# Two attention layers and the stage between them put into one block, with loads, weights and first steps moved inside the stage ahead

## The reference

```
x = x + L0_xattn(layernorm(x), ctx)   # attention, 16 heads of 16; every weight W becomes W + 2 * A @ B
x = x + sqrt(real^2 + imag^2)         # real = layernorm(x) @ cos(theta + theta_noise)
                                      # imag = layernorm(x) @ sin(phi + phi_noise)
x = x + L1_xattn(layernorm(x), ctx)   # attention, 16 heads of 16, queries and keys rotated by position
x = x + L1_ffn(layernorm(x))          # 256 -> 1024 -> 256, gelu, weights rounded to 8 bits, activations to 16
```

## Time and profile before

| what | us |
|---|---|
| median of 3 runs | 1995.51 (1990.53 to 1996.17) |
| the profiled execution | 1991.47 |
| its span, from the first instruction to the last | 1989.7 |
| busy: PE, DVE, ACT, POOL | 1665.4, 1316.0, 1219.0, 831.3 |
| granted TensorE clock, mean share of full speed | 0.91 |
| end of the chain of waits by engine: DMA, DVE, PE, ACT | 4%, 2%, 2%, 1% |

### The profile page before, as it was taken

One profiled execution on the slowest core, in us unless ns is written; L12 is line 12 of the kernel. 1 busy time (PEld: TensorE's weight loads), 2 busy tenths in 40 slices (PEclk: granted clock), 3 DMA queues, 4 the chain that ended last, 5 costly groups with the idle time before them and its releaser, 6 DMA issues. The chain is left out here.

```text
span 1989.7 us, 39510 instructions
## 1 busy us (share of the span) xinstructions
PE 1665.4 (84%) x13992; PEld 1259.2 (63%) x13992; DVE 1316.0 (66%) x2605; ACT 1219.0 (61%) x2189; POOL 831.3 (42%) x664
## 2 busy tenths in 40 slices
PE   0799999999999948957889999999989848884987
PEld 0567767766666526845666666666666526663987
DVE  5367776767777626853666676676776635776986
ACT  0166666666666518933666666666666527885975
POOL 0334554545545210025466566566566212221432
PEclk9889999999999858975989999999999768997999
DMA  6456676666666410025766776666776413556775
GB/s 193 89 127 153 154 155 147 150 146 153 145 151 154 95 39 0 0 73 109 148 143 140 149 147 142 145 151 142 151 150 132 94 42 127 219 221 278 254 250 194
DMA packets 152462, 281.25 MB, mean 141 GB/s; under 512 B 39888, under 2 KB 66128, under 8 KB 144080
## 3 DMA queue, kind: packets, MB, share of 16 engines
q1 hardware_dynamic: 152288, 278.96, 56.2%
HBM read 89.99 MB, written 59.77 MB: 75 GB/s over the span
## 5 line engine op out<-in xcount | busy, mean ns | idle before, releaser
L585 DVE TENSOR_REDUCE L_negm<-L_s_bank 128x2 f32<-128x512 f32 x1024 | 666.0, 684 | 431.3 <-PE L_s_bank L403 423.2
L506 ACT ACTIVATE L_prob<-L_t_bank 128x512 f32<-128x512 f32 x1024 | 576.6, 601 | 262.3 <-PE L_t_bank L419 255.0
L403 PE MATMUL L_s_bank<-L_kst,L_qst 48*128 48x256 f32 x2048 | 466.9, 333 | 45.9 <-DVE L_negm L585 33.6
L419 PE MATMUL L_t_bank<-L_qst,L_kst 50*128 50x256 f32 x2048 | 453.0, 328 | 24.6 <-DMA L_qst<-L_mT 20.6
L403 PEld LDWEIGHTS L_s_bank<-L_kst,L_qst 48*128 48x128 f32 x2048 | 309.7, 198 | 198.9 <-DVE L_negm L585 92.0
L419 PEld LDWEIGHTS L_t_bank<-L_qst,L_kst 50*128 50x128 f32 x2048 | 302.0, 196 | 43.4 <-DMA L_qst<-L_mT 25.3
L487 PE MATMUL L_eo<-L_prob,L_vext 128*17 128x256 f32 x4096 | 261.2, 391 | 5.4 <-ACT L_prob L506 5.3
L297 POOL TENSOR_TENSOR L_kqr<-L_kqr,L_cs 128x1024 f32<-128x1024 f32 x32 | 75.6, 2361 | 265.1 <-DMA L_kqr<-L_kq 265.1
L1219 PE MATMUL G_acc<-G_w_out,G_hhl 128*128 128x256 f32 x1024 | 134.4, 292 | 43.0 <-DVE G_hhl L1188 43.0
L487 PEld LDWEIGHTS L_eo<-L_prob,L_vext 128*17 128x17 f32 x4096 | 105.5, 99 | 102.5 <-issue 9.8
L516 ACT ACTIVATE L_osb<-L_eo 128x512 f32<-128x512 f32 x128 | 76.5, 598 | 145.6 <-PE L_eo L487 145.6
(11 more groups left out here) (155 smaller groups left out, 2661.5 us busy)
## 6 DMA issues: line engine op xcount, KB each, us to landing
L_kst<-L_hl SPq DMA_DIRECT2D x384, 128.0 KB, 3.5
L_qst<-L_hl SPq DMA_DIRECT2D x384, 128.0 KB, 4.3
hidden_scratch<-G_hid SPq DMA_DIRECT2D x32, 1024.0 KB, 3.9
G_hid<-hidden_scratch SPq DMA_DIRECT2D x32, 1024.0 KB, 7.4
c_scratch<-L_cT SPq DMA_DIRECT2D x32, 512.0 KB, 2.8
L_rb<-r_scratch SPq DMA_DIRECT2D x64, 256.0 KB
L_cT<-c_scratch SPq DMA_DIRECT2D x32, 512.0 KB, 3.3
L_kqr<-L_kq SPq DMA_DIRECT2D x64, 256.0 KB, 4.9
```

The lines of the kernel that those rows point to most:

```text
L403: mm = pe.matmul(s_bank[k % 2][:, t, :], qst[n % 2][rows, j, t, P * qt:P * (qt + 1)], kst[n % 2][rows, j, t, :], start=True, stop=True)
L419: mm = pe.matmul(t_bank[k % 2][:, t, :], kst[n % 2][rows, j, t, P * kt:P * (kt + 1)], qst[n % 2][rows, j, t, :], start=True, stop=True)
L506: act.activation(prob[h][:, kt, j, :, :], t_bank[k % 2][:, :, :], ACT.Exp, scale=HD ** -0.5).then_inc(sem["act_p"], 1)
L585: dve.tensor_reduce(negm[:, h, 0, :].rearrange("p (j t q) -> p j t q", j=HJ, t=KT)[:, j, :, qt], s_bank[k % 2][:, :, :], AX.X, ALU.max, ne ...
```

## The change

`start` disappears as a block. Layer 0, the middle stage and layer 1 become one block with one program for each engine, and one set of tiles (`Shared`) serves all three; the middle stage's tiles lie in tiles of the attention (`kst0`, `qst1`, `prob0`, `kq`, `kqr`) and its PSUM in `s_bank`, `t_bank` and `eo`. What ended a block is replaced by waits at the first use of each tile. In detail:

- SP loads 8 tiles of `x`, then weights, and the other 56 tiles in four DMAs after layer 0's second step; DVE takes their statistics in the head, between steps (14 tiles at a time). A square root and a reciprocal for these 56 tiles stand ahead of step 0.
- POOL splits two weights of layer 0 and all four of layer 1 (`high_low`).
- The angle tables are loaded ahead of layer 0's last step (31), and DVE reduces the angles in that step, at slot 4. Layer 0's drain steps 32, 33 and 34 stand ahead of turns -1, 1 and 3 of the middle stage. Batches 28 to 31 get their 1/sqrt at turn 5.
- The middle stage has one bank `tr` (it is `eo`) in place of two, and its loop is written out.
- Layer 1's weights, biases and rope table are loaded after layer 0's drain in SP's stream; PE, ACT and DVE take them up after turn 10. Layer 1's steps 28, 29 and 30 stand after turns 14, 20 and 26. The DMAs into `kst` and `qst` for batches 32 and 33 wait for the end of the middle stage, and the rows of ones come after the first of them.

```diff
-def attention(core, layer, sem, w, x_res, stats, extent, consts, src, scratch):
...
+def attention(core, layer, sem, f_sem, tiles, w, x_res, stats, extent, consts, src, scratch):
...
+    LOADED = (0, 8, 22, 36, 50, TILES)
...
+    def sync_rest_of_x(sp):
+        xt = src["x"].rearrange("b (t p) f -> p (b t) f", p=P)
+        for j in range(1, 5):
+            sp.dma_start(x_res[:, LOADED[j]:LOADED[j + 1], :], xt[:, LOADED[j]:LOADED[j + 1], :]).then_inc(sem[f"x_load{j}"], 16)
...
+                        after(sp, sem["pe_t"], 16 * (n - 2) + 8 * h + 8)
+                        after(sp, sem[f"stack{h}"], 96 * n)
+                        if rope and n <= lo + 1:
+                            sp.wait_ge(f_sem["pe_mm"], B)
+                            sp.wait_ge(f_sem["dve_x"], B)
+                        stack(n, h)
+                        if n == lo and h == 0:
+                            all_ones()
...
+    def high_low(eng, n, of):
+
+        eng.tensor_copy(whl[n][:, 0, :, :], of).then_inc(sem[f"whl_{n}"], 1)
+        eng.wait_ge(sem[f"whl_{n}"], 1)
+        eng.tensor_tensor(whl[n][:, 1, :, :], of, whl[n][:, 0, :, :].bitcast(F32), ALU.subtract).then_inc(sem[f"whl_{n}"], 1)
...
+            pool.wait_ge(sem["w_load"], weights)
+            for n in "qkvo":
+                high_low(pool, n, raw[n])
...
+    def vector_statistics(dve, j):
+
+        dve.wait_ge(sem[f"x_load{j}"], 16)
+        count = LOADED[j + 1] - LOADED[j]
+        after(dve, sem["x_stats"], j)
+        for t in range(count):
+            ins = dve.bn_stats(bst[:, t, :], x_res[:, LOADED[j] + t, :])
+        ins.then_inc(sem["x_bn"], 1)
+        dve.wait_ge(sem["x_bn"], j + 1)
+        for t in range(count):
+            ins = dve.bn_aggr(mvt[:, t, :], bst[:, t, :])
+        ins.then_inc(sem["x_ag"], 1)
+        dve.wait_ge(sem["x_ag"], j + 1)
+        dve.tensor_copy(stats[:, LOADED[j]:LOADED[j + 1], :], mvt[:, 0:count, :]).then_inc(sem["x_stats"], 1)
...
-def start(core, x, x_res, stats, consts, src):
...
-        per = TILES // LOADS
-        block = ctx.enter_context(nc.Block())
-
-        @block.sync
-        def _(sp):
-            xt = x.rearrange("b (t p) f -> p (b t) f", p=P)
-            for j in range(LOADS):
-                sp.dma_start(x_res[:, per * j:per * (j + 1), :], xt[:, per * j:per * (j + 1), :]).then_inc(sem[f"x_load{j}"], 16)
...
-        tr = [ps(f"tr{j}", [P, KT, S]) for j in range(2)]
-        ri = [ps(f"ri{j}", [P, NT, 2 * D]) for j in range(2)]
...
+def cos_sin_ffn(sem, l_sem, tiles, x_res, stats, consts, src):
...
+    width, batch = KT * 2 * D, NT * D
+    ang = tiles.kq[:, :, :, :]
+    noise = tiles.kqr[:, :, :, :]
+    cs = tiles.kqr[:, :, :, :].rearrange("p k j d -> p k (j d)")
+    cshl = flat(tiles.kst[0]).rearrange("p (c k d) -> p c k d", c=2, k=KT)
+    xT = [flat(tiles.qst[1])[:, width * j:width * (j + 1)].rearrange("p (c k s) -> p c k s", c=2, k=KT) for j in range(2)]
+    probs = tiles.prob[0][:, :, :, :, :].rearrange("p n j t s -> p (n j t s)")
+    sq = [probs[:, 2 * batch * j:2 * batch * (j + 1)].rearrange("p (t d) -> p t d", t=NT) for j in range(2)]
+    xn = [probs[:, batch * j:batch * (j + 1)].rearrange("p (t d) -> p t d", t=NT) for j in range(4, 6)]
+    mag = [probs[:, batch * j:batch * (j + 1)].rearrange("p (t d) -> p t d", t=NT) for j in range(6, 8)]
+    tr = tiles.eo
+    ri = [bank[:, :, :, :].rearrange("p n t s -> p n (t s)") for bank in (tiles.s_bank, tiles.t_bank)]
...
+    def sync_begin(sp):
+        sp.wait_ge(l_sem["pool_low"], B)
+        sp.wait_ge(l_sem["pool_c"], B)
...
+                    pe.wait_ge(l_sem["act_eo"], 2 * B)
...
-        start(core, a["x"], x_res, stats, consts, a)
...
+            DRAIN = {B: -1, B + 1: 1}
+            HEAD = {i: 14 + 6 * (i - l1.first) for i in range(l1.first, last)}
+            BEGIN, EIGHT = 10, 8
...
+            @block.sync
+            def _(sp):
+                l0_step, l1_step = l0.program[0](sp), l1.program[0](sp)
+                l0.begin[0](sp)
+                for i in range(l0.first, l0.end):
+                    if i == last:
+                        f0.begin[0](sp)
+                    l0_step(i)
+                    if i == l0.first + 1:
+                        sync_rest_of_x(sp)
+                l1.begin[0](sp)
+                for i in range(l1.first, l1.end):
+                    l1_step(i)
+
...
+            @block.tensor
+            def _(pe):
+                l0_step, l1_step, f0_step = l0.program[2](pe), l1.program[2](pe), f0.program[2](pe)
+                l0.begin[2](pe)
+                for i in range(l0.first, B):
+                    l0_step(i)
+                for j in range(f0.first, f0.end):
+                    for i in drains(j):
+                        l0_step(i)
+                    f0_step(j)
+                    if j == BEGIN:
+                        l1.begin[2](pe)
+                    for i in heads(j):
+                        l1_step(i)
+                for i in range(last, l1.end):
+                    l1_step(i)
...
+                    dve.memset(consts[n][:, :], value).then_inc(sem["const_set"], 1)
+                dve.wait_ge(sem["const_set"], 3)
+                l0.begin[4](dve)
+                for i in range(l0.first, last):
+                    if i == 0:
+                        l0_inverse(dve, 1, rest)
+                    l0_step(i)
+                    if i == l0.first + 1:
+                        for j in (1, 2):
+                            l0_statistics(dve, j)
+                    if i == l0.first + 2:
+                        for j in (3, 4):
+                            l0_statistics(dve, j)
+                l0_step(last, angles_at, f0.begin[4])
+                f0_variance(dve, 0)
+                angle_parts(dve)
+                f0_inverse(dve, 0)
+                for j in range(f0.first, f0.end):
+                    for i in drains(j):
+                        l0_step(i)
+                    if j == 5:
+                        f0_variance(dve, 1)
+                        f0_inverse(dve, 1)
+                    f0_step(j)
+                    if j == BEGIN:
+                        l1.begin[4](dve)
+                    for g in roots(j):
+                        l1_inverse(dve, g, slice(2 * EIGHT * g, 2 * EIGHT * (g + 1)))
+                    for i in heads(j):
+                        l1_step(i)
+                for i in range(last, l1.end):
+                    l1_step(i)
```

More of the change, by code:

```diff
@@ L1 @@
 from contextlib import ExitStack
+from dataclasses import dataclass
 import numpy as np
@@ new lines, in attention @@
+    ctx_in = [kqr[:, j, :, :] for j in range(2)]
+    raw = {n: prob[layer][:, layer, j, :, :] for j, n in enumerate("qkvo")}
+    lora_a = {n: prob[1][0:RANK, 0, j, 0, :] for j, n in enumerate("qkvo")}
+    lora_b = {n: prob[1][0:RANK, 1, j, 0, :] for j, n in enumerate("qkvo")}
+    ones = prob[1][32:34, 0, :, :, :]
+    bvx = osb[0][:, 0, :, 0:P]
+    KQ_HIGH, KQ_LOW = hl[:, 0:4:2, :, :], hl[:, 1:4:2, :, :]
+    nmr, rstd = stats[:, :, 0], stats[:, :, 1]
+    s_bank = [tiles.s_bank[:, j, :, :] for j in range(2)]
@@ new lines, in attention @@
+    t_bank = [tiles.t_bank[:, j, :, :] for j in range(2)]
+    eo, misc = tiles.eo, tiles.misc
+    bank = {n: misc[j] for n, j in BANK[layer].items()}
+    ident, eps = consts["ident"], consts["eps"]
+    r_dram, c_dram = scratch["r"], scratch["c"]
+    lo, hi = B * layer, B * (layer + 1)
+    sem = dict(sem, **core.sems(f"L{layer}", "b_load w_load rstd ones_set bvx ones0 pe_bo bo whl_q whl_k whl_v whl_o"
+                                + (" rot prod sum" if rope else " lora lora_w less v_set eo_set pick high_c"
+                                   " x_load0 x_load1 x_load2 x_load3 x_load4 ident")))
@@ new lines, in attention, with on, due, ready @@
+    place = PLACE[layer]
+    first, end = lo - max(a for a, _ in place.values()), hi - min(a for a, _ in place.values())
+    def on(n):
+        return lo <= n < hi
+    def due(op, i, k):
+        ahead, slot = place[op]
+        return [i + ahead] if slot == k and on(i + ahead) else []
+    biases = 16 * (4 if rope else 3)
+    weights = 16 * 4 * (1 if rope else 3)
+    lora_banks = (misc[0], misc[1], s_bank[0], s_bank[1])
+    LOADED = (0, 8, 22, 36, 50, TILES)
+    def ready(n):
+        return 3 * ((n - lo) // 8 + 1) if rope else 3 if 2 * n < LOADED[1] else 6
@@ L170, in attention @@
-        lo, hi = B * layer, B * (layer + 1)
-        sem = dict(sem, **core.sems(f"L{layer}", "b_load w_load wts less rstd ones_set v_set bvx eo_set ones0 pe_bo bo"
-                                    + (" rot prod sum" if rope else " lora high_c pool_c")))
-        block = ctx.enter_context(nc.Block())
-        place = PLACE[layer]
-        start_at, end_at = lo - max(a for a, _ in place.values()), hi - min(a for a, _ in place.values())
-        def drive(step):
-            for i in range(start_at, end_at):
-                step(i)
@@ L181, in on @@
[L181 to L205 removed]
```

(1 more changed line is left out.)

1313 lines of the change are left out of this document (676 added, 637 removed).

## The result

The changed kernel takes 1927.1 us (median; 1919.0 to 1928.2) and the kernel before, on the same chip, 1995.8 (1990.5 to 1997.5): ratio **0.9651, 95% interval 0.9619 to 0.9683**. Its profiled execution has a span of 1925.3 us, 64.4 less than before's 1989.7. The forecast was 1919, with 77 us off the span, and a range of 1903 to 1938.

The account below looks back on a forecast made before the run. PE is nearly full in layer 0's steps, PE and ACT in the middle loop, so time lies in the gaps: 31 + 28 - 20 + 38 = 77 us off, 1919 us from the median 1995.5; range 1903 to 1938.

Parts of the forecast that it names:

- The start: Load of x and layer 0's head: earlier first products, DVE's statistics still bounding; gain 31 us, bounds 24 and 40.
- Step 0 near 74: Sign for the start: layer 0's step 0 begins near 74 us, where it began at 105.33.
- The way into the loop: Layer 0's end to the middle stage's second product: angles and head work moved earlier; gain 28 us, bounds 24 and 31.
- The cover I asked for: Layer 0's end: batch 31's last y by 728.3, PE at its Wo at 728.9; each us after 729 is lost.
- The loop: Middle stage's loop, PE and ACT full: inserted bodies, bias, waits, transposes and roots cost 20 us, bounds 12 and 32.
- the second rival: Middle loop: POOL's rotation and weight splits bar DVE's additions, 14.4 us at most; 1931 us, chance 6%.
- the rule against it: Middle loop: the skill's rule that DVE two-SBUF-operand and reading GpSimd instructions exclude each other for their whole length; 6%.
- The way into layer 1: Middle loop's last addition to layer 1's first scores: 45.4 us falls to 7.6; gain 38, bounds 33 and 41.
- The first: Rival: middle loop loses its step after insertions, clock falls in waits; 12 to 20 us more, 1934, chance 15%.
- The third: Rival: at the start statistics are hidden because PE is later up to step 0; 5 to 9 more gained, 1911, 6%.
- The fourth: Rival: layer 1's head is placed in the loop but held back by a wait; 24 us less gained, 1943, chance 4%.
- fifth: Rival: the middle loop's single bank breaks the overlap, 2.8 us more a turn; slower at 2009 us, chance 3%.

Follow-up runs that it names:

- run 11: Changed kernel with all of x loaded ahead of the weights and all its statistics taken before layer 0's first step: 1943.5 us.
- run 2: Changed kernel with all three placed steps of layer 1 behind the middle loop's last product; weights, bias row and angles stay placed: 1924.4 us.
- run 3: Changed kernel with only layer 1's third placed step moved behind the middle loop's last product: 1918.9 us, ratio 0.9616.
- run 10: Changed kernel repeated unchanged, beside the kernel with three edits together: 1928.4 us, ratio 0.9662.
- run 1: Changed kernel repeated unchanged, for a second profile: 1927.8 us.
- run 4: Changed kernel with layer 1's third placed step and the first rotation (SP's copies, POOL's operations) behind the middle loop's last product: 1922.8 us.
- run 9: Changed kernel with third placed step behind the loop, PE's bias-row wait in turn 14, ACT's first-stack copy in turn 31: 1920.5 us, ratio 0.9620.
- run 6: Changed kernel with statistics of x's last 42 tiles moved from layer 0's head between the maxima of steps 0 to 2: 1931.5 us.

## Why the prediction was right, and where it was off

**The start.** Right in mechanism and nearly in size (31, measured 33.1): DVE's statistics bound the head without idle, and the first maxima start at 52.67 against 53.6. That this is so close is partly luck: the statistics began 1.7 us later than I put them (28.2, not 26.5), and with the second low part they took 24.4 us, not 27.1. "Step 0 near 74" came at 72.3. What I had not split is in run 11.

**The way into the loop.** 28, measured 29.9. The cover I asked for held by a hair: the last half of y was done at 695.20, and the last product with W_o starts at 695.55, as the first product of the loop ends.

**The loop.** This is the term that was mis-sized: 20, measured 28.2. By turns (over 3.21 us): two bodies 7.0 and 7.3, 14.4 (forecast 13); bias 3.1 and 1.6 on the lower clock behind it (3); the wait at turn 5 0.9 (2); transposes 0.4 and one visible root 0.2 (1.4); layer 0's drain and the weights' splits 2.2 (0); the rotation 5.7 (0), of which 1.5 is a turn on the lower clock behind it. The last two terms, 7.9 us at which I put nothing, hold the miss, and 7.2 of them are what the second rival named. The other two profiles of the unchanged text give the loop 129.5 and 128.2, so its cost is 26.7 to 28.2. **The failed step is my reading of the earlier trace rows.** I took 0.82 us beside a POOL instruction as 0.13 a piece, wrote that the two overlapped, and gave the rule against it 6%. The neighbours of that row in the timeline of the kernel before, which I left out, say otherwise:

```profile
871.61 0.40 POOL L291 COPY L_osb<-L_bvc 128x256 f32<-128x256 f32 x1 [4.03 <-DMA L_cs<-in_rope]
871.73 0.82 DVE L565 TENSOR_TENSOR L_wk<-L_prob,L_wk 128x512 fp32r<-128x512 f32 x1
871.99 2.46 POOL L305 TENSOR_SCALAR L_xn<-x_res,stats 128x256 f32<-128x256 f32 x2
```

POOL's copy lasted only 0.40 us, so DVE could lose no more than 0.28 to it; and POOL's two operations behind it took 2.46 us, where the same two take 1.10 alone (L371 in run 2, at 831.55): there POOL waited for DVE. The rows of the loop show the other reading: L879 starts at 781.27, POOL's product runs from 781.10 to about 783.5, and L879 ends 0.6 us after that. The Trainium skill (SBUF — State Buffer, "SBUF: two separate sides") calls the port pair that the two engines share an exclusive lock, held for the whole instruction, between a VectorE operation with two SBUF inputs and a GpSimd operation that reads SBUF. This case agrees: beside POOL's products 1.95 to 2.8 us for 0.69, and nothing more for the operation with an operand in PSUM.

**The way into layer 1.** 38, measured 37.9, and yet it was no gain of 38. I added it and the loop's cost as if they were separate; together they came to 9.7 us, not 18, and what belongs to what shows only in pairs. The three placed steps: 23.6 won, 20.2 to 21.8 paid. Weights, bias and angles: 14.7 won on the way (46.5 to 31.8), 4.4 paid in the loop (107.9 less 103.5), the best-placed part. The third step should have stood in TensorE's 10.7 us of idle time behind the loop, as run 3 shows (the 10.69 us ahead of 835.46).

**Layer 1's steps.** The forecast took nothing from them. The profile shows 8.4 us more (666.9 against 658.5), but the unchanged text gave 658.4 in run 10 and 665.0 in run 1, and the time goes with the granted clock: 0.90 with 665.0 and 666.9, 0.93 with 655.0 to 658.5 (runs 2, 4, 9, 10, and before). So no part of the 8.4 is shown to be the change's; there is only one profile of the kernel before to compare with. What makes one execution's clock lower is not shown by these runs.

**The sum and the range.** The 77 us off the span were 64.4: 8.2 too little for the loop and 8.3 behind it, less 2.1 and 1.9 that the start and the way into the loop won more. The measured 1927 is 8 above the forecast and inside the range. The stated 1903 to 1938 does not follow from "15 either side", which is 1904 to 1934.

**The rivals.** The first (engines out of step, and a lower clock in the waits) happened for a small part of its price of 12 to 20. Most long turns have a cause of their own and the turn behind them is 3.2 again, but two in the first profile are not: 4.79 behind the bias and 4.75 behind the rotation, at a granted clock of 0.64 and 0.65, 3.1 us together. The second (POOL bars DVE) happened, at half of its price of 14.4: 5.7 for the rotation and 1.5 for the weights. The third did not happen: DVE's statistics end at 52.67 with PE waiting, and run 6 shows that in steps 0 to 2 there is no free place for them either. The fourth and fifth did not occur: the turns were 3.21 with one bank `tr`.

## What to carry to other kernels

Work put into a loop that is full on two engines is paid there at full price; ask of each piece what it saves behind the loop, take the pieces apart in pairs, and put the last one into the idle time between the stages. Before placing work on an idle POOL, look for operations with two SBUF operands on DVE beside it: count whole instructions, not overlaps. When a few us are at stake, compare marks of the trace that lie between the same two instructions, because the same unchanged layer varied by 12 us with the clock.

## What the runs showed of the hardware

- POOL's 128x1024 product (2.4 us) made DVE's 128x512 addition of two SBUF tiles take 1.95 to 2.77 us instead of 0.69, and took 2.71 to 2.82 itself; with an operand in PSUM DVE's 0.65 stayed. A copy of 0.61 us on POOL made the addition take 1.08.
- A stretched addition can cost more than its own wait. In the changed kernel PE idled 1.55 us ahead of the turn at 785.31, whose product took 3.03, and 2.16 us ahead of the next, whose product took 4.56 at a granted clock of 0.65 (the row at 790.91). In run 1 PE idled as long in the same places (1.58 and 2.19 us) and both products took 3.00; the turn there is 3.2 us in runs 1 and 6 and 4.6 to 4.8 in the others that have the rotation in the loop.
- Layer 0, alike in all kernels here, took 605.6 to 617.8 us from step 0 to its last eviction (run 6 left out) at a mean granted clock of 0.97 to 0.94, and layer 1's 32 steps 655.0 to 666.9 at 0.93 to 0.90.
